# Last layer of a four-layer graph GRU kernel: roots for ten blocks, loops of 20 blocks, stored selections, two summed blocks in five with their own h

## The reference

```python
x = node_embed
for l in range(4):
    m = x @ weight[l]
    agg = jax.ops.segment_sum(m[src], dst, num_segments=n_nodes)
    x = _gru_cell(agg, x, w_ih, w_hh, b_ih, b_hh)
y = node_embed + (x + node_embed)
out = (y - mean(y)) / sqrt(var(y) + 1e-5)
```

## Time and profile before

| | |
|---|---|
| median of three runs | 2310.44 us (2309.59 to 2311.28) |
| the profiled execution | 2312.41 us, of which the profile's span is 2310.7 us |
| TensorE's granted clock, mean | 0.984 |
| PE busy | 2219.9 us (96%) |
| DVE busy | 2158.7 us (93%) |
| ACT busy | 1847.9 us (80%) |
| POOL busy | 1660.1 us (72%) |
| DMA | 362.44 MB, mean 157 GB/s |

### The profile page before, as it was taken

The page is one execution under the profiler, slowest core; times in us unless marked ns, Lnnn a source line. Parts: engine busy times, 40 slices in busy tenths (PEclk is TensorE's granted clock), DMA queues, the critical chain, the costliest instruction groups (busy, mean ns, idle before and its releaser), DMA issues.

```text
span 2310.7 us, 49242 instructions
## 1 busy us (share of the span) xinstructions
PE 2219.9 (96%) x11764; PEld 1909.5 (83%) x11764; DVE 2158.7 (93%) x4077; ACT 1847.9 (80%) x3483; POOL 1660.1 (72%) x1632
## 2 busy tenths in 40 slices
PE   3999999999999999999999999999989999999996
PEld 2888888888878888888878888888877888888885
DVE  7899999999979999999969999999979999999998
ACT  1688888888858888888857888888856888888887
POOL 3877777777577777777647777777748877777882
PEclk7999999999999999999999999999999999999998
DMA  2455555555545666566645665666553565555564
GB/s 58 114 156 161 160 159 158 161 160 160 152 134 168 172 173 173 171 172 171 171 122 166 174 173 171 172 173 173 172 161 98 158 162 164 160 164 159 164 162 119
DMA packets 277064, 362.44 MB, mean 157 GB/s; under 512 B 107755, under 2 KB 186587, under 8 KB 276981
## 3 DMA queue, kind: packets, MB, share of 16 engines
q1 hardware_dynamic: 238118, 309.12, 45.0%
q0 software_dynamic: 38784, 52.30, 10.2%
q10 hardware_dynamic: 78, 0.08, 0.0%
HBM read 208.71 MB, written 179.20 MB: 168 GB/s over the span
## 4 chain that ended last, share of the span: by engine, by line
PE 69%; DVE 17%; issue 9%; DMA 2%; ACT 1%; POOL 1%; DVEq 1%; POOLq 0%; ACTq 0%; SPq 0%
PE pZ L856 18%; PE pR L856 9%; PE pHN L856 9%; PE pA L844 9%; PE pO L938 5%; PE pA L856 4%; PE pIN L856 4%; PE pR L897 3%; PE pR L900 3%; PE pR L898 3%; DVE narg L1419 3%; DVE diff L1423 2%; DVE bn L1455 2%; DVE aggT L1393 2%; PE pH L787 2%
## 5 line engine op out<-in xcount | busy, mean ns | idle before, releaser
L692 POOL DMA_INDIRECT gath<-state,idx x900 | 942.5, 1047 | 263.7 <-issue 252.3
L675 POOL TENSOR_TENSOR h_lo<-hT,h_hi 128x500 fp32r<-128x500 f32 (+1 forms) x400 | 376.2, 941 | 236.1 <-ACT h_hi L1059 180.9
L692 POOL DMA_INDIRECT gath<-in_x_dram,idx x300 | 322.2, 1074 | 101.9 <-issue 70.1
L1090 ACT ACTIVATE rg<-pR,bsum 128x500 f32<-128x500 f32 x400 | 270.6, 676 | 116.4 <-PE pR L900 103.4
L1412 DVE SCALAR_TENSOR_TENSOR narg<-pHN,bhh,rg 128x500 f32<-128x500 f32 x400 | 292.6, 731 | 47.3 <-ACT rg L1090 45.9
L1071 ACT CAST sel<-sel 128x504 fp32r (+1 forms) x400 | 245.9, 615 | 31.6 <-DVE flag_i L1367 29.5
L1429 DVE TENSOR_TENSOR diff<-pZ,diff 128x500 f32<-128x500 f32 x400 | 268.0, 670 | 0.6
L1384 DVE TENSOR_TENSOR a_lo<-aggT,a_hi 128x500 fp32r<-128x500 f32 x378 | 258.3, 683 | 0.2
L1098 ACT ACTIVATE pZ<-pZ,bsum 128x500 f32<-128x500 f32 x400 | 256.4, 641 | 1.0 <-PE pZ L856 1.0
L1393 DVE TENSOR_TENSOR aggT<-pA,hT 128x500 f32<-128x500 f32 x378 | 252.4, 668 | 2.0 <-PE pA L844 1.8
L1094 ACT ACTIVATE pIN<-narg,bih 128x500 f32<-128x500 f32 x200 | 136.5, 683 | 120.3 <-DVE narg L1419 120.3
(11 more groups left out here) (219 smaller groups left out, 6377.7 us busy)
## 6 DMA issues: line engine op xcount, KB each, us to landing
columns<-newT SPq DMA_DIRECT2D x300, 250.0 KB, 2.3
hT<-columns SPq DMA_DIRECT2D x300, 250.0 KB, 2.8
state<-o_rows SPq DMA_DIRECT2D x300, 224.0 KB
x_rows<-in_x_dram SPq DMA_DIRECT2D x200, 224.0 KB
out_dram<-o_rows SPq DMA_DIRECT2D x91, 224.0 KB
gath<-state,idx POOLq DMA_INDIRECT x900, 2.5
state<-o_rows SPq DMA_DIRECT2D x297, 26.0 KB
idx<-edge_src SPq DMA_DIRECT2D x395, 1.5 KB
```

The costliest lines, as they stand in the source:

```text
L675: nc.gpsimd.tensor_tensor(part_of(h_lo, u)[:, cols], hT[:, u % RING, cols], part_of(h_hi, u)[:, cols].bitcast(F32), ALU.subtract).then_inc ...
L692: pool.indirect_dma_start(out=gath[:, u % RING, j, :], out_offset=None, in_=states[l], in_offset=bass.IndirectOffsetOnAxis(ap=idx[:, u % R ...
L1090: nc.scalar.activation(rg[:, :], pR[:, 0:COLS], ACT.Sigmoid, bias=bsum[:, 0:1]).then_inc(s_r, 1)
```

## The change

- **Batches of ten.** The roots are made for ten blocks at once (`BATCH`, `batch_done`), so the output lags 13 blocks, not 9. For the last ten steps `caught_up` and `rows_by` set how many rows ACT normalises: four in the steps of blocks 90 to 92, six in those of 93 to 99.
- **Loops of 20.** `UNROLL` is 20: each layer is 20 steps, a loop with three turns of 20 steps, 20 steps. y_rows grows to 20 slots, ten of which lie in the memory of sel8 (`y_slot`).
- **Selections loaded.** In layer 0 SP also stores each widened selection to DRAM (258 KB a block). In the last layer nothing is widened: SP loads them into five slots, which take the memory of sel, g_hi and g_lo; the first five in the last step of layer 2.
- **Own h.** `by_tensor` holds for blocks with u % 5 in (1, 4), so for 36 blocks, not 18.
- `r_times_hn` waits for HN only in the first step of all (later waits cover it).

```diff
-UNROLL = 10
+UNROLL = 20
+BATCH = 10
+OWN = (1, 4)
...
-OUTLAG = 9
+OUTLAG = BATCH + 3
...
-        g_hi = sb("g_hi", [P, 2, TILES, D], F32R)
-        g_lo = sb("g_lo", [P, 2, TILES, D], F32R)
-        sel = sb("sel", [P, 2, SELW], F32R)
+        mixed = sb("mixed", [P, max(2 * SELW + 2 * GATHERED, RING * SELW)], F32R)
...
+        sel_loaded = mixed[:, 0:RING * SELW].bitcast(F32).rearrange("p (t c) -> p t c", t=RING)
...
         def by_tensor(l, b, u):
-            return l == L - 1 and u % RING == 0 and not (isinstance(b, int) and b < UNROLL)
+            return l == L - 1 and u % RING in OWN and not (isinstance(b, int) and b < UNSPLIT)
...
-        def half_done(i, u, at):
-            if u % RING != at % RING:
+        def batch_done(i, u, lag):
+            first = u - lag - (BATCH - 1)
+            if isinstance(i, int) and i == GROUPS - 1 and first == 2 * BATCH - UNROLL + RING:
+                return slice(UNROLL - BATCH, UNROLL - RING), NB // BATCH - 1
+            if first % BATCH:
                 return None
...
+        def caught_up(i, u):
+            return isinstance(i, int) and i == GROUPS - 1 and u >= BATCH
+        def rows_by(u):
+            behind = RPP * (NB - UNROLL + BATCH - OUTLAG)
+            return behind + max(0, min(u - BATCH + 1, 3)) * RPP + max(0, u - BATCH - 2) * (RPP + 2)
...
+            def store_selection(b, u):
+                sp.wait_ge(s_sel, b + 1)
+                sp.nop(nofuse=True)
+                sp.dma_start(columns_of(selections, b), sel[:, u % 2, :].bitcast(F32)).then_inc(s_selst[u % 2], 16)
+            def load_selection(b, u, summed):
+                sp.wait_ge(s_pA, summed)
+                sp.nop(nofuse=True)
+                sp.dma_start(sel_loaded[:, u % RING, :], columns_of(selections, b)).then_inc(s_selld[u % RING], 16)
...
+                        if l == 0 and exists(i, u, 2):
+                            store_selection(*after(i, u, 2)[:2])
+                        if l == L - 1 and exists(i, u, RING):
+                            load_selection(b + RING, u, l * NB + b + 1)
+                        if l == L - 2 and last:
+                            for c in range(RING):
+                                load_selection(c, c, (l + 1) * NB)
...
             def widen(l, b, u, i=0):
                 if l == 0:
                     act.wait_ge(s_sel8, b + 1)
+                    if not isinstance(b, int) or b > 1:
+                        act.wait_ge(s_selst[u % 2], 16 * (UNROLL // 2 * i + u // 2))
...
                     def normal(i, u, part):
-                        if final and exists_before(i, u, lag):
+                        if final and caught_up(i, u):
+                            middle = rows_by(u - 1) + 2
+                            halves = range(rows_by(u - 1), middle, 2) if part == 0 else range(middle, rows_by(u), 2)
+                            for r in halves:
+                                c = r // RPP
+                                normalise(c % UNROLL, TURNS * l + c // RING, batch(GROUPS - 1, c - (NB - UNROLL)) + 1,
+                                          r % RPP // 2)
...
-                        if final and not ramp and exists(i, u, 3):
-                            widen(l, *after(i, u, 3)[:2])
```

More of the change, by code:

```diff
@@ L321, in build @@
         s_sel = sem("selection_widened")
+        s_selst = [sem(f"selection_stored_{u}") for u in range(2)]
+        s_selld = [sem(f"selection_loaded_{u}") for u in range(RING)]
         s_pA = sem("edges_summed")
@@ L518, in fast_path @@
                         indices(c, c)
+                    if l == 0:
+                        for c in range(2):
+                            store_selection(c, c)
                     def step(i, u, first, last):
@@ L549, in step @@
                             load_columns(l, b + RING, u)
-                        if l == L - 1 and exists_before(i, u, OUTLAG):
+                        if l == L - 1 and not caught_up(i, u) and exists_before(i, u, OUTLAG):
                             store(l, *after(i, u, -OUTLAG)[:2])
+                        if l == L - 1 and caught_up(i, u):
+                            for c in range(rows_by(u - 1) // RPP, rows_by(u) // RPP):
+                                store(l, c, c % UNROLL)
+                        if l == 0 and exists(i, u, 2):
[5 more added lines that the diff above has]
+                                load_selection(c, c, (l + 1) * NB)
                         if l < L - 1 and not exists(i, u, RING):
@@ L1155, in step @@
                         if first:
-                            for c in range(2):
+                            for c in range(0 if final else 2):
                                 widen(l, c, c)
@@ L1191, in step @@
                         normal(i, u, 1)
-                        if ramp and u != 1:
+                        if ramp and u != 1 and not final:
                             widen(l, {0: 2, 2: 5, 3: 6}[u], {0: 2, 2: 5, 3: 6}[u])
@@ L1518, in renew @@
                         again = not (isinstance(t, int) and t == 0 and l == 0)
-                        new_state(l, b, u, (TURNS * l + t if not final else TURNS * l) if again else None,
+                        if final:
+                            stored = TURNS * l if isinstance(b, int) and b < RING else None
+                        else:
+                            stored = TURNS * l + t if again else None
+                        new_state(l, b, u, stored,
                                   g - RING + 1 if again else None)
@@ L1550, in step @@
                             aggregate(l, 4, 4)
-                        r_times_hn(l, b, u)
+                        r_times_hn(l, b, u, first and l == 0)
                         if not ramp and not last:
@@ L1601, in step @@
                             low_part(l, 5, 5)
-                        if opening(i) and not unsplit(l, b + 3):
+                        if opening(i, u) and not unsplit(l, b + 3):
                             low_gathered(l, *after(i, u, 3)[:2])
```

136 lines of the change are left out of this document (83 added, 53 removed).

## The result

The changed kernel takes **2325.23 us** (median of 4 runs, 2322.90 to 2325.98), the kernel before beside it 2310.86 us: a ratio of 1.0064, 95% interval 1.0050 to 1.0077, so slower by 14.4 us. The forecast was 2315.5 (2307 to 2327), slower with 0.50. The sign and the range held. The measured time lies 9.7 us above the forecast, for the most part by one rival's cost, which I had given 0.25. The forecast's own range, 2309 to 2322, would not have held; the stated one reaches to 2327 because of that rival.

A forecast was written before the change was run, and what follows sets the result against it. DVE was taken as the bound, by 0.42 us in 27.78 over PE, with PE the bound after the change. Terms 2.1 + 2.4 + 3.0 - 1.9 - 0.5 = +5.1 us gave 2315.5 us against the median, range 2307 to 2327.

The forecast's parts named there:

- Steady steps: Last layer, blocks 10 to 98: PE becomes the bound at 27.82 us per five steps; +2.1 us if PE never waits.
- ACT without its cast: Last layer: the selection's cast leaves each step, but ACT already had 0.41 us idle ahead of the tanh, so no gain.
- Last ten steps: Last layer's end: extra rows put ACT's ring at 6.0 to 6.1 us, above PE's 5.56; +2.4 us, between 0.5 and 4.
- Boundary: Layer 2 to 3: five selection loads ahead of the stores delay the first gathers; +3.0 us, between 0 and 5.
- The sign named for this term: Layer 2 to 3: the last layer's first gather about 3 us later behind the end of layer 2.
- First steps: Last layer's start: less PE waiting for POOL's h_lo, and roots once POOL has caught up; -1.9 us, between -4 and 0.
- Layer 0, 0: Layer 0: each selection's store lands 1.1 us before the cast that overwrites its slot, so it costs nothing.
- the casts of layer 0 wait for DMA: Layer 0: listed among the observations that would prove the prediction wrong.
- Loops, -0.5: All layers: five turns fewer in each, a branch taking 0.056 us; -0.5 us, between 0 and -1.1.
- if a branch takes microseconds: Loop jumps: listed among the observations that would prove the prediction wrong.
- The loop rival: Loops: the longer body no longer stays where instructions are fetched from; eight jumps back, about +8 us, 2323.5; chance 0.25.
- Not in the sum: Layers 1 and 2: the forecast had 0 for this stretch.

The follow-up runs named there:

- e11_dve_straight: The changed kernel with only VectorE's last layer written out, the other engines keeping their loop of twenty there: 2314.17 us, ratio 1.0020 to the kernel before.
- e8_before20_own2: e3_before20 with TensorE adding the own h in two blocks of five, not one: 2314.36 us, ratio 1.0019 to the kernel before.
- e12_even: The changed kernel normalising four rows, not six, in each of the last seven steps: 2328.16 us, ratio 1.0072 to the kernel before.
- e1_straight: The changed kernel with its last layer written out for all engines, without jumps back there: 2316.56 us, ratio 1.0028 to the kernel before.
- e3_before20: The kernel before with loops of twenty blocks and nothing else of the change: 2309.95 us, ratio 0.9997 to the kernel before.
- e9_before20_straight: e3_before20 with its last layer written out, without jumps back there: 2306.46 us, ratio 0.9987 to the kernel before.
- e10_before20_sel: e3_before20 with selections stored in layer 0 and loaded in the last layer: 2315.59 us, ratio 1.0028 to the kernel before.

## Why the prediction was right, and where it was off

Part of it was luck. Without VectorE's reload the change is still slower, by 4.0 us (e11_dve_straight), near the +5.1 of my sum. But the terms in it were off in both directions and made this up between them: steady steps and layer 0 cost 2.3 us each more than I had, the boundary 1.6 less, and layers 1 and 2, where I had nothing, took 4.1 us less.

- **Steady steps, +2.1: mechanism right, size short.** "PE is now the bound, at 27.82" per five steps: 27.75 without roots, 27.80 in e8_before20_own2. What failed is "the roots come once in ten blocks (half of 1.16, -0.58)". I counted them as time that DVE saves, and gave the wait in the step behind them as an upper bound, 0.3 us once in ten, +2.5. Per ten steps it is 0.47 in the loops and 0.3 in the last group, so steps 20 to 40 are 1.1 us longer, not 0.2. Steps 10 to 98 take 506.2 us; without 6.9 for the jumps and 1.4 for the six rows that is +4.4 over the 493.5 of before.
- **ACT without its cast, 0:** right; only the kernels with selections stored and loaded show a cost, and not here.
- **Last ten steps, +2.4:** right. Steps 90 to 98 take 2.1 us more (49.23 and 51.31). ACT's ring of 6.0 to 6.1 us was too long, though: the steps with six rows take 5.64 to 5.87 us, so that only three of them stand out (and 97 by 0.06), and by e12_even the six rows hold 1.4 of my 1.9 us. The rest is own h and roots.
- **Boundary, +3.0:** half right. The gather is as late as I said, 7.25 us behind the step's first matmul and not 4.32 (+2.9). "PE waits all of it" is what failed: once issued, the gather reaches PE in 3.2 us, before in 4.7, so that PE waits 1.4 us longer. The sign named for this term, the late gather, would have passed as proof of the 3.0. Not foreseen: that moving the loads would gain nothing in this step.
- **First steps, -1.9:** -1.2, and not for the reason given. Step 8 alone takes 6.97 us, not 10.00, and the others give 1.9 back. In the kernel before, PE's wait of 2.41 us had a second price that I did not see, 3.4 us at clock 0.50:

```profile
1780.80:1784.10 3.30, 3.17 (x10) 2.94 (x11) 3.27 (x9) 0.95 (x2) 2.55 (x3) 0.50 0.12 26
```

  In the changed kernel PE's longest wait in steps 1 to 9 is 1.34 us, and the clock stays at 1.00. The sign that I named, no DVE instruction of over 1 us in the first 15 steps, failed: DVE's timeline has

```profile
1756.45 1.71 DVE L1467 TENSOR_TENSOR a_lo<-aggT,a_hi 128x500 fp32r<-128x500 f32 x1
...
1780.38 2.43 DVE L1467 TENSOR_TENSOR a_lo<-aggT,a_hi 128x500 fp32r<-128x500 f32 x1
```

  Both overlap an h_lo of POOL. In this trace seven of the 372 a_lo made from aggT overlap one, and these seven take 1.01 to 2.43 us, all others at most 0.73. The collisions with POOL moved from a root to a_lo.
- **Layer 0, 0: failed behind the two jumps.** The "1.1 us of margin" held for the ordinary step of this trace: steps 20 to 40 are as long as before. But I took SP's queue as always on time. Behind a jump it is 3 to 4 us late, and steps 40 to 80 pay 2.3 us. The sign "the casts of layer 0 wait for DMA" came true. The margin is thin elsewhere too: in seven of the nine other kernels that store selections, a cast near 207 us, with no jump ahead of it, waits 0.8 to 1.5 us for its store, and in three of them steps 20 to 40 are 0.4 to 1.0 us longer.
- **Loops, -0.5: the step that failed.** I priced a jump by the branch's own length, 0.056 us, and the sign that I named, "if a branch takes microseconds", would not have caught it: the branches of the loops still take 0.056 us. The loop rival had the mechanism: two jumps on VectorE in the last layer cost 3.0 and 3.9 us (against step 20 to 40 of the same kernel), 6.9 in all, and 8.7 by e1_straight and 11.1 by e11_dve_straight in the medians. Its sum, 2323.5, is 1.7 from the measured time, but it had eight jumps at about 1 us; only two cost, each three times that. Against the rival I had held that none of 32 branches took longer, which says nothing about a body twice as long. That was weak evidence, and it deserved less weight than the doubling.
- **Not in the sum:** -4.1 us in layers 1 and 2. e3_before20 shows 2.8 of it and e9_before20_straight, the same code in these layers, 1.2; the spread between executions is as large as the effect. In this trace 3.3 us of it lie in layer 2's first 20 steps, where the kernel before was granted 0.50 twice for 3.4 us, the changed one once.

The medians' 14.4 us in parts, by the runs, each with 2 to 3 us of uncertainty, and added as if they did not act on each other, which no run shows: loops of twenty alone -0.3, the second own h +4.4 (its trace has most of it at the jumps), stored and loaded selections +5.6; this makes 9.7, and the other 4.7 is left for the roots for ten blocks (0.4 for each ten steps, eight times: 3.2) and the six-row steps (1.4). These two are from the traces. With VectorE's last layer written out, e11_dve_straight, 4.0 us of the 14.4 remain.

## What to carry to other kernels

In these kernels each engine had its own length of loop body beyond which a jump back stopped it for 2.6 to 5.0 us, and this showed as "issue" idle time behind the branch, not in the loop's branch (56 ns). The one long branch record, PE's way out of the fast path, is no loop's. Before you lengthen a body, count each engine's instructions per turn, look for instruction packets in the DMA view of the loop, and write out the engine that is critical. Here, with two engines within 2% of each other, the roots spread over every five blocks cost less than fewer of them in one lump. And the five loads stood in the way of the gather ahead of it on the queue as well as beside it on the DMA engines; moving them by a few us swapped one for the other. Where a change adds or removes a long wait of PE, look at the granted clock behind it.

## What the hardware showed that I had not expected

- VectorE reloaded with turns of 400 recorded instructions (3.4 to 5.0 us in 400 to 453) and not with 301 to 337, nor with the 169 to 235 of the kernel before. The longer turn was not the dearer one: 453 took 3.4, 400 took 4.2 and 5.0.
- SP's limit is no plain count: with 371 recorded instructions it stopped for 2.9 to 3.2 us in layer 1 of the changed kernel and not in layer 2 (0.28), while in e3_before20, with the same 371, it stopped in both (3.6 to 3.8 and 3.1 to 3.2). ACT (up to 302), POOL (up to 166) and PE never did.
- The Trainium skill, Runtime: NRT & Kernel Launch, Instruction fetch mechanics, has the instruction memory of an engine as two blocks of 256 instructions, refilled in sequence, and TensorE's four times as large; a taken branch out of this window stalls. The runs agree in kind. By that, a turn between one block and two stays or not by where it starts, which would fit 371 instructions that stall in one layer and not in the next. One pair of runs bears on it: e10_before20_sel has SP's body of layer 2 from e3_before20, and longer code ahead of it (472 recorded instructions a turn in layer 0, not 391). In e3_before20 that body stops for 3.1 and 3.2 us, in e10_before20_sel for 0.3. So it goes by where the body lies and not by its length alone; that blocks of 256 are the reason is argued. What is shown is that VectorE was safe up to 337 here and not at 400, short of 512.
- Whether a loop fetches code can be read from the DMA view of a window over it: no packet of queue 14 in the last layer's loop before, 23 in 1961 to 2190 of the changed kernel. The page's total (141 and 52 packets) does not tell it, since e1_straight, without a jump in the last layer, has 127.
- Straight code shows no cost here: e9_before20_straight runs through 100 steps of the last layer, and PE is busy for 102.00 of the 102.00 us shown.
- The last layer's first step varied with TensorE's clock as much as with the loads: behind its first sums it took 6.4 us at clock 1.00 (e3_before20) and 8.1 with 5.8 us of it at 0.50 (before).
